# A graph network in one kernel: attention layers in blocks of 512 queries, value rows streamed, output turned back in two steps

## The reference

```python
def _gat_layer(x, W, adj):
    proj = x @ W
    Wh, Ws = jnp.split(proj, 2, axis=-1)
    scores = Wh @ Ws.T
    a = jax.nn.softmax(scores, axis=-1) * adj
    out = a @ Wh
    out = out + x
    return jax.nn.leaky_relu(out, NEG_SLOPE)
...
h = jnp.maximum(_layernorm(x, axis=-1), 0.0)
x = x + _L1_gnn_ref(h, adj, L1_gnn_W_stack)      # two _gat_layer, one after the other
```

## Time and profile before

| | |
|---|---|
| median of 3 runs | 2601.47 us (2601.43 to 2603.41) |
| the profiled execution's own time | 2604.16 us |
| span in its trace, first to last instruction | 2602.4 us |
| TensorE busy | 2496.5 us (96%), 18492 products |
| VectorE, ScalarE, GpSimd busy | 84%, 65%, 59% |
| mean granted TensorE clock | 0.989 of full |
| DMA | 248.21 MB, mean 95 GB/s |

### The profile page before, as it was taken

How to read it: one execution, slowest core, us unless ns; L and a number is a source line. 1 busy time by engine, 2 the same in 40 slices (tenths; PEclk the granted TensorE clock), 3 DMA queues, 4 the chain that set the end, 5 groups by cost and what they waited for, 6 DMA issues and landing times. The chain is left out here.

```text
span 2602.4 us, 47910 instructions
## 1 busy us (share of the span) xinstructions
PE 2496.5 (96%) x18492; PEld 2363.2 (91%) x18492; DVE 2190.1 (84%) x2917; ACT 1685.2 (65%) x2316; POOL 1523.0 (59%) x932
## 2 busy tenths in 40 slices
PE   7699999999999979999999999987999999999997
PEld 5588888888888869999999999987999999999997
DVE  5899999999999647888888898894788888888888
ACT  5999999999999655555555555553555555555554
POOL 4899999999999702444444444450345444444446
PEclk9799999999999989999999999999999999999999
DMA  3332322232323031333333233233233333333333
GB/s 110 115 94 90 94 90 93 90 93 90 93 90 94 13 104 49 98 94 105 94 101 103 90 106 98 90 114 110 66 94 118 98 101 115 97 103 110 102 99 105
DMA packets 100979, 248.21 MB, mean 95 GB/s; under 512 B 9360, under 2 KB 51088, under 8 KB 100752
## 3 DMA queue, kind: packets, MB, share of 16 engines
q1 hardware_dynamic: 98880, 243.30, 30.5%
q10 hardware_dynamic: 1872, 1.84, 0.2%
HBM read 232.52 MB, written 12.58 MB: 94 GB/s over the span
## 5 line engine op out<-in xcount | busy, mean ns | idle before, releaser
L91 PE MATMUL l0b_acc<-l_h_parts,l0b_turned_hi 128*128 128x512 f32 x1984 | 727.2, 406 | 19.6 <-POOL l0b_turned_lo L579 19.5
L579 POOL TENSOR_TENSOR l0b_turned_lo<-l0b_turned,l0b_turned_hi 128x1024 fp32r<-128x1024 f32 x256 | 614.3, 2415 | 44.7 <-ACT l0b_turned_hi L616 42.8
L92 PE MATMUL l0b_acc<-l_h_parts,l0b_turned_lo 128*128 128x256 f32 x1984 | 558.4, 281 | 0.0
L1171 POOL TENSOR_TENSOR g0b_sum_wide<-g0b_sum_wide,g0b_slab 128x512 f32<-128x512 f32 x240 | 311.2, 1297 | 396.5 <-DVE g0b_masked_psum L1279 386.4
L1171 POOL TENSOR_TENSOR g1b_sum_wide<-g1b_sum_wide,g1b_slab 128x512 f32<-128x512 f32 x240 | 315.5, 1315 | 339.5 <-DVE g1b_masked_psum L1279 328.7
L91 PEld LDWEIGHTS l0b_acc<-l_h_parts,l0b_turned_hi 128*128 128x128 f32 x1984 | 376.1, 190 | 112.8 <-POOL l0b_turned_lo L579 29.7
L92 PEld LDWEIGHTS l0b_acc<-l_h_parts,l0b_turned_lo 128*128 128x128 f32 x1984 | 374.2, 189 | 0.9
L616 ACT CAST l0b_turned_hi<-l0b_turned 128x1024 fp32r<-128x1024 f32 x256 | 268.1, 1047 | 67.4 <-PE l0b_acc L92 50.3
L80 PE MATMUL g0b_acc<-g_wh_parts,g0b_part_hi 128*128 128x256 f32 x1024 | 293.6, 287 | 6.8 <-DVE g0b_part_lo L1285 5.7
L80 PE MATMUL g1b_acc<-g_wh_parts,g1b_part_hi 128*128 128x256 f32 x1024 | 293.6, 287 | 5.6 <-DVE g1b_part_lo L1285 4.5
L80 PE MATMUL g0b_score_psum<-g0b_q_block,g_vt_hi 128*128 128x256 f32 x1024 | 290.3, 284 | 2.5 <-DVE g0b_q_block L1315 1.4
(11 more groups left out here) (234 smaller groups left out, 7221.2 us busy)
## 6 DMA issues: line engine op xcount, KB each, us to landing
g_adj_ring<-in_adj_blocks_dram SPq DMA_DIRECT2D x256, 512.0 KB, 3.6
l_adj_ring<-in_adj_quads_dram SPq DMA_DIRECT2D x128, 512.0 KB, 3.6
l0b_x_in<-in_x_dram SPq DMA_DIRECT2D x32, 128.0 KB, 2.4
x_rows<-l0b_x SPq DMA_DIRECT2D x32, 128.0 KB, 2.3
g0a_rows<-x_rows SPq DMA_DIRECT2D x8, 512.0 KB, 5.4
g0b_y<-x_rows SPq DMA_DIRECT2D x16, 256.0 KB, 4.0
v_rows<-g0b_y SPq DMA_DIRECT2D x16, 256.0 KB, 4.5
g1a_rows<-v_rows SPq DMA_DIRECT2D x8, 512.0 KB, 5.0
```

Of the source, the lines that this page charges most:

```text
L91: pe.matmul(out, lhs_hi, rhs, start=first, stop=False)
L92: return pe.matmul(out[:, width:], lhs_lo, rhs[:, :width], start=False, stop=False)
L579: pool.tensor_tensor(turned_lo[:, m % PART_RING, :, :], turned[:, m % TURN_RING, :, :], turned_hi[:, m % PART_RING, :, :].bitcast(F32), AL ...
L1171: pool.tensor_tensor(sum_wide[:], sum_wide[:], half_of(c, e), ALU.add).then_inc(summed, 1)
```

## The change

Only `attention_layer` is changed, and the layout of one input.

- BLOCK is 512 queries and CHUNK 2 tiles, so a chunk holds as many elements as before and a layer has 128 chunks as before, but a block has PER = 16 chunks, and the three distances are 17, 18 and 19 steps in place of 9, 10 and 11.
- All products of part b are 512 columns wide. `weigh` swaps its operands: the value rows are stationary and the attention is moving, so `acc` holds features on partitions and has to be turned back: ScalarE copies it to SBUF (`copy_out`), TensorE turns it in two groups of four transposes one step apart (`turn_out`), VectorE scales each (`drain`), and ScalarE applies the slope (`leak`, on VectorE before).
- The value rows no longer fit in SBUF beside 19 slab slots. Part a stages each quad of `wh` in two buffers and stores it to DRAM (1 MB each, `store_wh`); part b reads 512 KB of it in each step beside the 512 KB of adjacency (`fetch_wh`). SyncE issues both.
- Scores, queries, turned maxima, turned sums and turned outputs share one ring of three PSUM banks (`turns_of_step`); each use waits until the use three turns before has been read. The folds of maximum and sum are gone, since a bank is one tile wide.

```diff
-    BLOCK = 256
+    BLOCK = BANK
...
-    CHUNK = 4
+    CHUNK = 2
...
-    SLOTS = 11
+    SLOTS = PER + 3
...
+                    def store_wh(c):
+                        sp.wait_ge(out_lo_made, OUTS * (c + 1))
+                        wait(sp, wh_stored, 16 * c)
+                        stage = wh_stage[:, (c % 2) * OUTS:(c % 2 + 1) * OUTS, :, :, :].bitcast(F32)
+                        sp.dma_start(wh_dram[:, c, :], stage.rearrange("p o t h d -> p (o t h d)")
+                                     ).then_inc(wh_stored, 16)
...
                     def out_high(c):
+                        wait(act, wh_stored, 16 * (c - 1))
...
+            COPY_OUT, TURN_OUT, DRAIN = TURN_SUM + 1, (TURN_SUM + 2, TURN_SUM + 3), TURN_SUM + 4
...
+            def turns_of_step(n):
+                b = block_at(n, Q_AT)
+                if b is not None and b + 1 < BLOCKS:
+                    yield from (("query", KT * (b + 1) + m) for m in range(KT))
+                if n < CHUNKS:
+                    yield "score", CHUNK * n
+                for k in range(2):
+                    b = block_at(n, TURN_OUT[k])
+                    if b is not None:
+                        yield "out", 2 * b + k
+                for kind, offset in (("max", TURN_MAX), ("sum", TURN_SUM)):
+                    b = block_at(n, offset)
+                    if b is not None:
+                        yield kind, b
+                if n < CHUNKS:
+                    yield "score", CHUNK * n + 1
...
+                    def fetch_wh(c):
+                        wait(sp, products, c - ADJ_SLOTS + 1)
+                        sp.dma_start(wh_ring[:, c % ADJ_SLOTS, :, :, :].rearrange("p t h d -> p (t h d)").bitcast(F32),
+                                     wh_by_chunk[:, c % PER, :]).then_inc(chunk_in[c % ADJ_SLOTS], 16)
...
+                    def copy_out(b):
+                        act.wait_ge(products, PER * (b + 1))
+                        wait(act, out_turned, 2 * b)
+                        act.copy(turned_out[:], acc[:]).then_inc(out_copied, 1)
...
-                        for i in range(SUBS):
-                            cols = slice(i * P, (i + 1) * P)
+                        for d in range(KT):
+                            cols = slice(d * P, (d + 1) * P)
                             last = three_products(
-                                pe, acc[:, i, 0:D], (part_hi[:, c % 2, q, cols], part_lo[:, c % 2, q, cols]),
-                                (wh_parts[:, j, 0, :], wh_parts[:, j, 1, :]), j == 0, j == T - 1)
+                                pe, acc[:, d, :],
+                                (wh_ring[:, c % ADJ_SLOTS, e, 0, cols], wh_ring[:, c % ADJ_SLOTS, e, 1, cols]),
+                                (part_hi[:, c % 2, e, :], part_lo[:, c % 2, e, :]), j == 0, j == T - 1)
```

More of the change, by code:

```diff
@@ L1127, in block_at, with bank, tile_of @@
                 return b if rest == 0 and 0 <= b < BLOCKS else None
+            def turns_of_step(n):
[14 more added lines that the diff above has]
+                    yield "score", CHUNK * n + 1
+            order = [("query", m) for m in range(KT)] + [use for n in range(ENDS) for use in turns_of_step(n)]
+            turn_of = {use: turn for turn, use in enumerate(order)}
+            def bank(kind, k):
+                return side_psum[:, turn_of[kind, k] % BANKS, :]
+            def tile_of(c, e):
+                return slab[:, c % SLOTS, e, :]
             with nc.Block() as block:
@@ L1208, in q_high @@
                     def q_high(b):
-                        act.wait_ge(q_made, b + 1)
-                        wait(act, score_made, HALVES * (b - 1))
-                        act.copy(q_block[:, b % 2, 0, :, :], q_bank(b)).then_inc(q_hi_made, 1)
+                        for m in range(KT):
+                            act.wait_ge(q_made, KT * b + m + 1)
+                            if m == 0:
+                                wait(act, score_made, CHUNK * PER * (b - 1))
+                            act.copy(q_block[:, b % 2, 0, m, :], bank("query", KT * b + m)).then_inc(q_hi_made, 1)
                     def normalise(b):
@@ L1222, in _ @@
                         if 1 <= n <= CHUNKS:
[L1223 removed]
+                            take_tile(n - 1, 1)
                         b = block_at(n, Q_AT)
@@ L1318, in _ @@
                     q_low(0)
-                    for n in range(STEPS + 1):
-                        turning, drained = block_at(n, TURN_MAX), block_at(n, TURN_SUM + 1)
-                        if drained is not None:
-                            drain(drained)
+                    for n in range(ENDS):
                         if 0 <= n - TO_SPLIT < CHUNKS:
@@ L1326, in _ @@
                             join_max(n - 1, 1)
-                        if turning is not None:
-                            fold_max(turning)
+                        for k in range(2):
+                            b = block_at(n, TURN_OUT[k])
+                            if b is not None:
+                                drain(b, k)
                         if 0 <= n - TO_SHIFT < CHUNKS:
@@ L1342, in _, with wait_for_bank @@
                             totals(b)
-                        if drained is not None:
-                            leak(drained)
+                        if n < CHUNKS:
+                            join_max(n, 0)
                 @block.tensor
                 def _(pe):
-                    def wait_for_bank(turn):
-                        before = turn - SCORE_BANKS
-                        if before in half_at:
-                            pe.wait_ge(score_taken, half_at[before] + 1)
-                        if before in q_at:
-                            pe.wait_ge(q_lo_made, q_at[before] + 1)
+                    def wait_for_bank(kind, k):
+                        turn = turn_of[kind, k]
+                        if turn < BANKS:
+                            return
+                        last_kind, j = order[turn - BANKS]
+                        if last_kind == "score":
+                            pe.wait_ge(score_taken, j + 1)
+                        elif last_kind == "query":
+                            pe.wait_ge(q_lo_made, j + 1)
+                        elif last_kind == "max":
+                            pe.wait_ge(neg_step, 3 * j + 1)
+                        elif last_kind == "sum":
+                            pe.wait_ge(total_step, 2 * j + 1)
+                        else:
+                            pe.wait_ge(scaled, 2 * (j + 1))
@@ L1404, in turn_sum, with turn_out @@
                                                 ident)
                         last.then_inc(sum_turned, 1)
-                    def weigh(c, q):
+                    def turn_out(b, k):
+                        pe.wait_ge(out_copied, b + 1)
+                        wait_for_bank("out", 2 * b + k)
+                        for i in range(SUBS // 2):
+                            here = slice((k * SUBS // 2 + i) * P, (k * SUBS // 2 + i + 1) * P)
+                            for d in range(KT):
+                                last = pe.transpose(bank("out", 2 * b + k)[:, i * D + d * P:i * D + (d + 1) * P],
+                                                    turned_out[:, d, here], ident)
+                        last.then_inc(out_turned, 1)
```

304 lines of the change are left out of this document (156 added, 148 removed).

## The result

The changed kernel takes 2663.12 us (median of 4 runs, 2661.91 to 2663.82) against 2601.68 (2601.43 to 2603.41): a ratio of 1.0232, 95% interval 1.0219 to 1.0244. It is 61.4 us slower; the forecast was 94 us slower (2696, range 2640 to 2745). The profiled execution took 2661.91 us, its span is 2660.1.

The account below looks back on a forecast made before the run. The prediction took TensorE alone to pace the middle of the layers. Its terms, -15 + 15 + 10 + 46 + 22 + 16 = +94 us, gave a median of 2696 us, range 2640 to 2745.

Parts of the forecast that it names:

- its sign: Whole kernel: slower, chance 0.85; faster had 0.13 and no change 0.02.
- Width of the products: Paced stretches of both layers: 512-wide products start 0.2375 us apart, two 256-wide ones 0.240; -15 us, bounds -79 and 0.
- my lower bound: Paced products: with a fixed 0.013 us for each product, a 512-wide one takes 0.2265 us; gain bound -79 us.
- The ring of banks: Steps that turn an output: TensorE's next score waits 1.8 us, 24 times; with the turned maximum +46 us, bounds 0 and +58.
- A longer pipeline and the ends: Two terms: eight more fill and tail steps a layer, +15 us; last drains, copies, stores and residual at layer ends, +16 us.
- a bound (19): Tail steps without scores: late value-row reads could cost up to 0.5 us in each of 19, +19 us more.
- Reads of the value rows: Part b's steps: 512 KB more per step; landing may take 8.8 us before TensorE waits, so 0 us.
- Stores: Part a: eight 1 MB stores, one after another, 5.2 us each plus 0.2 to issue; +22 us, bounds 0 and +87.
- my chain of seven periods: Part a, layer one: from first value rows at 944.5, seven store periods of 5.4 us end at 982.3; +9.6 us.
- TensorE's added transposes: Six blocks a layer: two groups of four transposes, 0.43 us each, while scores still run; +10 us.
- the rival on width: Paced products: 512-wide ones take 0.213 us, sum falls 144 to 2552; decides faster from 0.2215 downward; chance 0.13.

Follow-up runs that it names:

- half-width scores: Changed kernel with query and score products issued as two halves of 256 columns, output products still 512 wide: 2698.47 us, ratio 1.0370 to the kernel before.
- four stages: Changed kernel with part a's value rows stored through four stages of their own, two stores under way at once: 2653.92 us, ratio 1.0201 to the kernel before.
- three stages: Changed kernel with three store stages, two stores under way, first adjacency loads behind the stores: 2646.01 us, ratio 1.0167 to the kernel before.
- no reads: Changed kernel reading value rows back for only a layer's first three chunks, so its output is incomplete: 2656.12 us, ratio 1.0204 to the kernel before.

## Why the prediction was right in its sign and 33 us too high

- **Width of the products: mechanism as in my lower bound, and this is the term that was mis-sized.** I took 0.2375 us from the first block's 512-wide rows; in the layers it is 0.227, where the lower bound had 0.2265. Of the earlier trace rows the 0.013 over the columns' own time does belong to each product: 0.107 + 0.013 and 0.213 + 0.013. The term is 5880 x (0.240 - 0.227) = -76 where I had -15, and half-width scores give it back. The first block's rows misled because their pairs of widths 512 and 256 read as proportional; why products there start 0.235 apart I did not test, though the 0.231 beside half-width scores hints that taking turns with 256-wide products is a part of it. The Trainium skill (page "TensorE: Matmul & The Clock Gate", section "Back-to-back issue gap") has two figures for 512: by its rule columns / 2.4 + 2.5 ns, which it calls the gap of an isolated product, 216 ns, and for a stream that loads weights for each product about 131 ns. This kernel's is such a stream, and the measured 227 ns agrees with neither; it lies 11 above the first and 10.5 below mine.
- **The ring of banks: right, in place, number and size.** 24 stalls, 1.67 to 1.80 us in the profile's idle column and 1.83 to 1.96 by the starts, against 1.8; by the block periods they cost 49 us in all, against 46; the drain waits as described, up to 4.0 us. Moving the one drain takes them away.
- **Missing: the clock.** The stalls also brought the granted clock to 0.5 for eight products in 7 of 12 blocks, about 12 us. No row of the kernel before had a stall in part b's middle, so none could show it.
- **A longer pipeline and the ends: sizes short by some 10 us.** Fill, tail and exit come to +141 us in the table, where the same working (19 steps of 2.85, and tail steps of 3.82 with the drains' wait) gives some 130. The tail steps are 3.84 as expected. Late value rows there cost some 7 us, for which I had named a bound (19) and counted 0. I have not placed the rest.
- **Reads of the value rows: right** in the middle, where they cost nothing; landing in 4.1 us.
- **Stores: right in size, in layer one by luck.** +9.6 and +10.4 us against +9.6 and +12.1. In layer two it is as I said: each store waits for the one before, 4.9 to 5.2 us apart, against 5.2 + 0.2. In layer one my chain of seven periods is not what happens: up to the sixth store the row loads behind the stores set a period of 5.1 that comes out alike, one store is held up for 8.45 us by adjacency loads, and the sum meets mine by chance.
- **TensorE's added transposes: right.** In the block of 92.63 us, 2.7 are not products; of the two blocks before, 96.75 - 792 x 0.12 = 1.7. Added: 1.0 a block, 0.86 forecast.

In sum: -61 for the width, +12 for the clock, +3 for the stalls, +7 for late rows in the tail and +6 that I cannot place give -33. That the miss is no larger is luck: with the width put right and nothing else, my sum would have been 2635, below my range, and 28 too low. The sign held because the break-even of the rival on width, 0.2215, lay below the 0.227 that came. That left little room: with the one drain behind the join, the same change is 4 us faster than the kernel before.

## What to carry to other kernels

When two uses share a small ring of banks, ask for each reader's release what stands ahead of it in its engine's own order: a drain that waits for another engine belongs behind the operation that frees a bank. That one move was worth 65 us. A per-product cost read in another part of the program, where widths take turns, need not hold for a stream of one width: the fixed part was hidden there and decided 61 us here. And for a stream of stores, ask at each step what is waited for last: two under way helped where a store waited for the one before, and did nothing where a load behind it set the pace. Its buffers belong where the next stage does not at once need them.

## What the runs showed of the hardware that I had not expected

- A float32r product with its own weights costs its columns at 2.4 GHz and 13 ns more: 0.120 for 256, 0.227 for 512. The same shape starts 0.231 apart on average beside half-width scores, and 0.235 in the first block.
- A single stall of TensorE of 1.77 to 1.8 us in otherwise full work was followed by eight products at a granted clock of 0.5 in 22 of 36 cases (three kernels), and in 41 of 72 with the kernels of four stages, three stages and no reads (6, 6 and 7 of 12). Stalls of 1.67 to 1.71 us at the second place were not, in 72 cases, nor stalls of 1.63 to 1.74 in 24 with half-width scores. Length and place alone do not settle it, since 31 stalls of the same length at the same place had no drop; what decides stays open.
- Stores of 1 MB one after another took 4.9 us (median). Issued 3.3 to 4.6 us apart, in layer two of the kernel with three stages, they landed in 3.8 to 5.9. A 512 KB row load issued 0.4 us behind such a store landed in 5.9 us, where it took 3.6 to 3.8 without one.
